# Gate and up with stationary weights in an expert layer: no transposes of the product, down right behind its own up

## The chip, the cores and the metric

One core of a Trainium2 chip runs the whole program. The metric is the device time of one launch in microseconds. TensorE is PE here (PEld are its weight loads), VectorE DVE, ScalarE ACT, GpSimd POOL, and SyncE SP, which only issues transfers.

## What is computed

```python
x = x + _L0_ffn_ref(_L0_cond_ref(x, itok_B_1_198, L0_cond_weights), gate_w, wg, wu, wd)
x = x + _L1_ffn_ref(_L1_cond_ref(x, W, A, Bm, scalings, itok_B_0_6), base_w, base_b, router_w, router_b, lora_A, lora_B)

# _L0_ffn_ref: E = 64 experts, K = 8 of them per token, H = 1024, I = 384, CAP = 256 slots per expert
probs = softmax(x @ gate_w.T);  w, sel = top_k(probs, K);  w = w / sum(w)
inp = the first CAP tokens of each expert                      # (64, 256, 1024)
h = silu(einsum('ech,ehi->eci', inp, wg)) * einsum('ech,ehi->eci', inp, wu)
out = einsum('eci,eih->ech', h, wd)
y[token] += w * out
```

x is (32, 128, 1024) in fp32: 4096 tokens. The change touches the middle part, the 64 experts; the second layer (a product W x base_w, adapters and LoRA) is only touched where it begins.

## The kernel before

Every large product is made of three: each fp32 operand is split into a high half (a copy to float32r, made by ACT) and a low half (the rest, by a subtraction on DVE), and high x high, high x low and low x high are summed in PSUM. PSUM has 8 banks of 512 fp32 columns per partition (`bank(b, a, z)`).

**Order of the program.** Routing and conditioning of 32 token tiles come first (to about 198 us into the span), then the 64 experts (to about 1886 us), then the products for the second layer and its 32 tiles. Nothing reorders at run time: each engine runs its own list in the order written, and semaphores (`wait_ge`, `then_inc`) tie the lists together. So the loops in the five blocks (`block.sync`, `gpsimd`, `tensor`, `scalar`, `vector`) are the schedule.

**Weights of an expert** come in six units of 768 KB: gA, uA, gB, uB (halves of gate and up) and dA, dB (halves of down). `stream` and `units` set their order, down's one expert behind gate and up. SP loads them into four raw buffers (`load_unit`, L305; load n waits until the low half of unit n - 4 is done). ACT's `split` (L876) copies a unit to HR (eight slots; it waits by `wait_retired`, L272, until the matmuls have used the slot's last unit), and DVE's `split` (L1176) writes the rest to LR, 1536 columns each.

**Tokens of an expert.** POOL fetches, by indirect transfers, the expert's table rows (`gather_tab`, L472, 2 transfers), its tokens (`gather_x`, L485, 8 transfers: c = 0, 1 is the half of 128 tokens, q a quarter of the columns), its routing weights (`gather_w`, 2), and adds results to the output (`scatter`, L512, 2). DVE makes token numbers (`token`, L1219) and, with a small PE matmul (`repeat`, L635), row numbers (`index`, L1195). DVE turns the gathered blocks (`turn_x`, L1182), ACT makes their high half (`high_x`, L883), DVE the low half (`low_x`, L1189). `column` (L1235) copies the routing weight out of what was gathered.

**Gate and up** (`up`, L654): for each k of 8 and each half c, six matmuls of 384 columns: the tokens (XH, XL) are stationary, the weights (HR, LR) move. The result has tokens on the partitions. ACT takes `silu` (L893), DVE multiplies (`product`, L1210). **Turning the product** (`turn_h`, L646): six PE transposes of 128 x 128 into PSUM; ACT reads the high half (`high_h`, L888), DVE the low half (`low_h`, L1203). **Down** (`down`, L681): 4 results of 9 matmuls of 512 columns, banks 4 and 5 in turn; ACT scales each into `ot` (`result`, L899). PE's order is up(e), down(e - 1), turn_h(e).

**After the experts** PE turns base_w (`turn_b`, L698, 17 steps, ACT's `high_b` and DVE's subtraction after each, L1286 to L1296), nine steps before the last down and eight behind it, and then multiplies (L751).

Of the kernel before, what the change touches and what calls it, by code (L numbers as in the profile page):

```python
# [5 lines left out]
F32 = mybir.dt.float32  # L6
# [27 lines left out]
NB0 = 9  # L34
# [18 lines left out]
def adaln_ffn_kernel(nc, x, cond, adap, w0, gate_w, wg, wu, wd, W, A, Bm, scal,  # L53
# [14 lines left out]
    with ExitStack() as ctx:  # L68
# [38 lines left out]
        hH = sb("hH", [P, 2, 3, P], F32R, moe)  # L107
        hL = sb("hL", [P, 2, 3, P], F32R, moe)
# [5 lines left out]
        sil = sb("sil", [P, 2, I], F32, moe)  # L114
        prod = sb("prod", [P, 2, 3, P], F32, moe)
# [38 lines left out]
        XH = sb("XH", [P, 2, 2, 8, P], F32R, moe)  # L154
        XL = sb("XL", [P, 2, 2, 8, P], F32R, moe)
# [66 lines left out]
        s_H, s_L, s_k, s_dn = sem("s_H"), sem("s_L"), sem("s_k"), sem("s_dn")  # L222
        s_f, s_fh, s_fl = sem("s_f"), sem("s_fh"), sem("s_fl")
# [33 lines left out]
        stream(["gA", "uA", "gB", "uB"], 0)  # L257
        for e in range(1, E):
            stream(["gA", "uA", "gB", "uB"], e)
            stream(["dA", "dB"], e - 1)  # L260
        stream(["dA", "dB"], E - 1)

        def unit_src(n):
            k, e = units[n]
            h = 0 if k[1] == "A" else UN
            if k[0] == "d":
                v = wd[e].rearrange("(p j) h -> p (j h)", j=3)
            else:
                v = (wg if k[0] == "g" else wu)[e].rearrange("(p k) i -> p (k i)", k=8)
            return v[:, h:h + UN]  # L270
# [10 lines left out]

        fq = {}
        for e in range(2):
            fq[("i", e)] = len(fq)
        for e in range(E):
            if e + 2 < E:
                fq[("i", e + 2)] = len(fq)
            for c in range(2):
                fq[("h", e, c)] = len(fq)
# [7 lines left out]
        def _(eng):  # L297
# [7 lines left out]
            def load_unit(n):  # L305
                if n >= NRAW:
                    eng.wait_ge(s_L, n - NRAW + 1)
                eng.dma_start(raw[:, n % NRAW, :], unit_src(n)).then_inc(d_raw[n % NRAW], 16)
# [136 lines left out]
        def _(eng):  # L445
# [79 lines left out]
            gather_x(0)  # L525
            gather_x(1)
            gather_tab(2)
            gather_w(0)
            gather_w(1)
            for e in range(E + 1):  # L530
                if e + 3 < E:
                    gather_tab(e + 3)
                if e + 2 < E:
                    gather_x(e + 2)
                    gather_w(e + 2)
                if e >= 1:
                    scatter(e - 1)
# [35 lines left out]
        def _(eng):  # L573
# [61 lines left out]
            def repeat(e):  # L635

                q = fq[("i", e)]
                if q >= 2:
                    eng.wait_ge(s_fl, q - 1)
# [829 lines left out]
```

## Time and profile before

| | us |
|---|---|
| median of 3 runs | 2518.43 (2515.33 to 2520.38) |
| the profiled execution's own time | 2506.1 |
| span of its trace | 2504.4 |

| engine | busy us | share of the span | instructions |
|---|---|---|---|
| PE | 2427.9 | 97% | 13439 |
| PEld | 2283.1 | 91% | 13439 |
| DVE | 1620.9 | 65% | 2673 |
| ACT | 1123.1 | 45% | 1459 |
| POOL | 1535.2 | 61% | 1044 |

Busy time is a union: two overlapping instructions of one engine count once. The mean duration of a matmul is longer than the distance to the next one's start, since they overlap; PE's pace is read from starts. "Idle before" is the time in which an engine waited, and the arrow names what ended the wait.

### The profile page before, as it was taken

To read this page: it belongs to the slowest core of one execution; us is meant where nothing else is said; L and a number is where in the kernel's file an instruction comes from. 1 tells how busy PE (TensorE), PEld (TensorE's weight loads), DVE (VectorE), ACT (ScalarE), POOL (GpSimd) and SP (SyncE) were. 2 spreads that over 40 slices of the span, in tenths; PEclk is the share of its full clock that TensorE was granted. 3 is DMA by queue.
4 is the path that set the end of the run, shared out by engine and by line. 5 is a ranking of instruction groups with operands and counts; after the bars stand their busy time and mean duration, and the time that the engine had idled before them with its cause. 6 is when DMAs were issued, how large, how long until landed. Compare 5 with 4: busy or idle time off the path is not lost.

```text
span 2504.4 us, 35281 instructions
## 1 busy us (share of the span) xinstructions
PE 2427.9 (97%) x13439; PEld 2283.1 (91%) x13439; DVE 1620.9 (65%) x2673; ACT 1123.1 (45%) x1459; POOL 1535.2 (61%) x1044
## 2 busy tenths in 40 slices
PE   8966999999999999999999999999989999999998
PEld 6756999999999999999999999999979999999998
DVE  4665777777767777776777777677732155555554
ACT  4544555555555555555555555555532121111110
POOL 4017888888888888888888888888710032223221
PEclk9987999999999999999999999999999999999999
DMA  9976999999999999899998989899964244444441
GB/s 327 355 254 241 296 273 277 263 285 263 278 289 272 278 262 284 263 280 272 269 281 263 284 262 281 271 270 280 273 154 110 68 128 132 136 129 128 126 116 52
DMA packets 216026, 583.67 MB, mean 233 GB/s; under 512 B 82793, under 2 KB 105322, under 8 KB 215730
## 3 DMA queue, kind: packets, MB, share of 16 engines
q1 hardware_dynamic: 148658, 402.26, 48.6%
q0 software_dynamic: 55808, 160.28, 26.5%
q10 hardware_dynamic: 11392, 18.88, 2.0%
q8 instruction: 107, 1.75, 0.3%
q14 instruction: 61, 0.50, 0.1%
HBM read 460.97 MB, written 124.53 MB: 234 GB/s over the span
## 4 chain that ended last, share of the span: by engine, by line
PE 88%; DMA 2%; POOL 1%; DVE 1%; SPq 1%; issue 1%; ACT 0%; DVEq 0%; POOLq 0%; ACTq 0%
PE ps L674 41%; PE ps L694 20%; PE ps L800 16%; PE ps L751 5%; PE ps L784 2%; PE ps L651 2%; POOL Xg L498 1%; PE ps L765 1%; SPq L361 1%; DMA x<-in_L_ffn_base_w 0%; DMA Xg<-yd,idx 0%; PE ps L643 0%; DMA Wg<-wdr,toki 0%; DMA G<-tabd,rowi 0%; POOL Wg L508 0%
## 5 line engine op out<-in xcount | busy, mean ns | idle before, releaser
L498 POOL DMA_INDIRECT Xg<-yd,idx x512 | 862.4, 1684 | 166.9 <-issue 138.1
L1179 DVE TENSOR_TENSOR LR<-raw,HR 128x1536 fp32r<-128x1536 f32 x384 | 666.2, 1749 | 75.1 <-ACT HR L881 74.9
L881 ACT ACTIVATE HR<-raw 128x1536 fp32r<-128x1536 f32 x384 | 563.1, 1484 | 5.9 <-PE ps L674 2.3
L674 PE MATMUL ps<-HR,XH 128*128 128x384 f32 x2048 | 531.9, 340 | 11.3 <-DVE XL L1191 11.3
L674 PE MATMUL ps<-LR,XH 128*128 128x384 f32 x2048 | 521.5, 335 | 0.0
L674 PE MATMUL ps<-HR,XL 128*128 128x384 f32 x2048 | 521.1, 335 | 0.0
L674 PEld LDWEIGHTS ps<-HR,XH 128*128 128x128 f32 x2048 | 363.7, 189 | 11.4 <-issue 11.4
L674 PEld LDWEIGHTS ps<-LR,XH 128*128 128x128 f32 x2048 | 371.0, 188 | 0.0
L674 PEld LDWEIGHTS ps<-HR,XL 128*128 128x128 f32 x2048 | 371.0, 188 | 0.0
L694 PE MATMUL ps<-HR,hL 128*128 128x512 f32 x768 | 302.5, 394 | 0.0
L694 PE MATMUL ps<-HR,hH 128*128 128x512 f32 x768 | 301.2, 392 | 0.3 <-ACT ot L904 0.3
L694 PE MATMUL ps<-LR,hH 128*128 128x512 f32 x768 | 298.3, 388 | 0.0
L520 POOL DMA_INDIRECT accd<-ot,toki x128 | 203.9, 1593 | 94.7 <-ACT ot L904 57.5
L904 ACT ACTIVATE ot<-ps,wcol 128x512 f32<-128x512 f32 x256 | 176.4, 690 | 176.7 <-PE ps L694 176.0
L885 ACT ACTIVATE XH<-XR 128x1024 fp32r<-128x1024 f32 x128 | 135.0, 1055 | 259.7 <-DVE XR L1186 259.7
L481 POOL DMA_INDIRECT G<-tabd,rowi x128 | 168.6, 1318 | 129.1 <-DMA tabd<-ct 90.4
L551 POOL DMA_INDIRECT m8a<-m8d,midx x32 | 27.6, 864 | 323.0 <-PE ps L765 322.5
L897 ACT ACTIVATE sil<-ps 128x384 f32<-128x384 f32 x128 | 55.9, 489 | 310.8 <-PE ps L674 310.8
L800 PE MATMUL ps<-MH,xTH 128*128 128x392 f32 x768 | 185.1, 349 | 3.9 <-DVE xTL L1363 3.9
L800 PE MATMUL ps<-MH,xTL 128*128 128x392 f32 x768 | 180.0, 343 | 0.0
L800 PE MATMUL ps<-ML,xTH 128*128 128x392 f32 x768 | 179.7, 342 | 0.0
L694 PEld LDWEIGHTS ps<-LR,hH 128*128 128x128 f32 x768 | 144.2, 188 | 32.2
(169 smaller groups left out, 3212.9 us busy)
## 6 DMA issues: line engine op xcount, KB each, us to landing
raw<-in_L_ffn_wg SPq DMA_DIRECT2D x128, 768.0 KB, 6.1
raw<-in_L_ffn_wu SPq DMA_DIRECT2D x128, 768.0 KB, 6.8
raw<-in_L_ffn_wd SPq DMA_DIRECT2D x128, 768.0 KB, 6.5
xt<-in_x SPq DMA_DIRECT2D x32, 512.0 KB, 7.0
yd<-yrow ACTq DMA_DIRECT2D x32, 512.0 KB, 6.6
x<-accd SPq DMA_DIRECT2D x32, 512.0 KB, 4.9
out<-osb SPq DMA_DIRECT2D x32, 512.0 KB, 3.0
accd<-xt SPq DMA_DIRECT2D x24, 512.0 KB, 6.6
```

What stands on the lines that cost most here:

```text
L481: eng.indirect_dma_start(G[:, e % 2, c, :], None, tab, bass.IndirectOffsetOnAxis(ap=rowi[:, c * E + e:c * E + e + 1], axis=0))\
L498: eng.indirect_dma_start(Xg[:, c, q, :], None, yd4, bass.IndirectOffsetOnAxis(ap=idx4[:, e % 4, i:i + 1], axis=0))\
L520: eng.indirect_dma_start(acc, bass.IndirectOffsetOnAxis(ap=toki[:, c * E + e:c * E + e + 1], axis=0), ot[:, c, :], None, compute_op=ALU.ad ...
L674: mm = eng.matmul(bank(2 * c + g, 0, I), X[:, e % 2, c, k, :], Wt[:, s, o:o + I], start=(k == 0 and m < 2), stop=(k == 7 and m >= 4))
L694: mm = eng.matmul(bank(4 + h), X[:, c, j, :], Wt[:, s, f:f + 512], start=(j == 0 and m == 0), stop=(j == 2 and m == 2))
L751: mm = eng.matmul(bank(b0 + g, 0, z - a), X[:, j % 2, q, :], Y[:, q, a:z], start=(q == 0 and m == 0), stop=(q == 7 and m == 2))
L800: mm = eng.matmul(bank(b0 + n, 0, 392), X, Y[:, k, a:a + 392], start=(k == 0 and m == 0), stop=(k == 7 and m == 2))
L881: eng.activation(HR[:, (n + 2) % NHL, :], raw[:, n % NRAW, :], ACT.Copy).then_inc(s_H, 1)
L885: eng.activation(XH[:, e % 2, c, :, :].rearrange("p j (q t) -> p q j t", q=4), XR[:, c, :, :, :], ACT.Copy).then_inc(s_vh, 1)
L897: eng.activation(sil[:, c, :], bank(2 * c, 0, I), ACT.Silu).then_inc(s_sl, 1)
L904: eng.activation(ot[:, c, h * 512:(h + 1) * 512], bank(4 + h), ACT.Copy, scale=wcol[:, c * E + e:c * E + e + 1]).then_inc(s_out, 1)
L1179: eng.tensor_tensor(LR[:, (n + 2) % NHL, :], raw[:, n % NRAW, :], HR[:, (n + 2) % NHL, :].bitcast(F32), ALU.subtract).then_inc(s_L, 1)
```

## The change

- **Gate and up.** The weights are stationary, 128 of an expert's 384 columns at a time (block b of 3), and the tokens move: XX holds, for each k, the high half of all 256 tokens beside their low half. `wh` moves all 512 columns, `wl` the 256 of the high half. Per block 2 x 8 x 2 = 32 matmuls. Gate and up use banks 0, 1 or 2, 3 in turn. The result has the inner dimension on the partitions, so `turn_h` and its six transposes are gone.
- **After a block**, n = 3e + b: ACT copies the right half of both banks (`copy_2`), DVE adds the left half (`join`), ACT takes silu, DVE multiplies (`product`), ACT makes the high half (`high_h`), DVE the low half (`low_h`), all on 128 x 256 but the first two (128 x 2 x 256).
- **Down** runs right behind its own up, its units come with it. The loop over the 3 blocks is outermost, with four banks (4 to 7) open, so that block j is wanted only at step j. down's weights are read in the order (j p) h, in runs of 512 numbers.
- **Orders.** ACT, DVE and POOL loops are rewritten; POOL's scatter(e - 1) goes ahead of gather_x(e + 2), and gather_tab(2) ahead of gather_x(1). `repeat` uses banks 4 and 5 and waits for two results of expert e - 3. The base turns of the last expert stand inside its down.

```diff
+        for e in range(E):
+            stream(["gA", "uA", "gB", "uB", "dA", "dB"], e)
...
             if k[0] == "d":
                 eng.wait_ge(s_dn, 4 * (e + 1))
             else:
-                eng.wait_ge(s_k, 2 * e + (1 if k[1] == "A" else 2))
+                eng.wait_ge(s_up, 3 * (e + 1))
...
+            gather_tab(2)
             gather_x(1)
-            gather_tab(2)
...
                 if e + 3 < E:
                     gather_tab(e + 3)
+                if e >= 1:
+                    scatter(e - 1)
                 if e + 2 < E:
                     gather_x(e + 2)
                     gather_w(e + 2)
-                if e >= 1:
-                    scatter(e - 1)
...
+            def up(e):
+                eng.wait_ge(s_vl, 2 * e + 2)
+                for b in range(3):
+                    n = 3 * e + b
+                    if n >= 2:
+                        eng.wait_ge(s_gs, n - 1)
+                    for g, kind in enumerate("gu"):
+                        out = 2 * (n % 2) + g
+                        for k in range(8):
+                            u = pos[(kind + ("A" if k < 4 else "B"), e)]
+                            if b == 0 and k % 4 == 0:
+                                eng.wait_ge(s_L, u + 1)
+                            s, o = (u + 2) % NHL, (k % 4) * I + b * P
+                            wh, wl, xx = HR[:, s, o:o + P], LR[:, s, o:o + P], XX[:, e % 2, k, :]
+                            if k == 0:
+                                eng.matmul(bank(out), wh, xx, start=True, stop=False)
+                                eng.matmul(bank(out, 0, CAP), wl, xx[:, 0:CAP], start=False, stop=False)
+                            else:
+                                eng.matmul(bank(out, 0, CAP), wl, xx[:, 0:CAP], start=False, stop=False)
+                                mm = eng.matmul(bank(out), wh, xx, start=False, stop=(k == 7))
+                        if g == 0 and b == 0 and 0 < e < E - 2:
+                            repeat(e + 2)
+                    mm.then_inc(s_up, 1)
...
+            def down(e):
+                eng.wait_ge(s_fl, min(e + 3, E))
+                eng.wait_ge(s_L, pos[("dB", e)] + 1)
                 for j in range(3):
+                    eng.wait_ge(s_hl, 3 * e + j + 1)
+                    for o in range(4):
+                        c, h = divmod(o, 2)
+                        if j == 0 and e:
+                            eng.wait_ge(s_out, 4 * (e - 1) + o + 1)
+                        s = (pos[("dA" if h == 0 else "dB", e)] + 2) % NHL
+                        for m, (X, Wt) in enumerate([(hH, HR), (hL, HR), (hH, LR)]):
+                            mm = eng.matmul(bank(4 + o), X[:, j, c * P:(c + 1) * P], Wt[:, s, j * 512:(j + 1) * 512],
+                                            start=(j == 0 and m == 0), stop=(j == 2 and m == 2))
+                        if j == 2:
+                            mm.then_inc(s_dn, 1)
+                        if e == E - 1 and j >= 1:
+                            turn_b(8 * (j - 1) + 2 * o)
+                            turn_b(8 * (j - 1) + 2 * o + 1)
...
             for e in range(E):
                 up(e)
-                if e >= 1:
-                    down(e - 1)
-                for c in range(2):
-                    turn_h(e, c)
...
+            def copy_2(n):
+                eng.wait_ge(s_up, n + 1)
+                if n:
+                    eng.wait_ge(s_hp, n)
+                b0 = 2 * (n % 2)
+                eng.activation(gu[:, :, :], ps[:, b0:b0 + 2, CAP:2 * CAP], ACT.Copy).then_inc(s_c2, 1)
+
+            def silu(n):
+                eng.wait_ge(s_gs, n + 1)
+                eng.activation(sil[:, :], gu[:, 0, :], ACT.Silu).then_inc(s_sl, 1)
+
+            def high_h(n):
+                e, b = divmod(n, 3)
+                eng.wait_ge(s_hp, n + 1)
                 if e:
+                    eng.wait_ge(s_dn, 4 * e)
+                eng.activation(hH[:, b, :], prod[:, :], ACT.Copy).then_inc(s_hh, 1)
...
+            split("dA", 0)
+            for e in range(E):
+                split("dB", e)
+                if e + 1 < E:
+                    high_x(e + 1, 0)
+                    high_x(e + 1, 1)
+                copy_2(3 * e)
+                silu(3 * e)
+                high_h(3 * e)
                 if e + 1 < E:
                     split("gA", e + 1)
                     split("uA", e + 1)
+                for b in (1, 2):
+                    copy_2(3 * e + b)
+                    silu(3 * e + b)
+                    high_h(3 * e + b)
+                if e + 1 < E:
                     split("gB", e + 1)
                     split("uB", e + 1)
+                    split("dA", e + 1)
+                    for o in range(4):
+                        result(e, o // 2, o % 2)
...
+            def join(n):
+                b0 = 2 * (n % 2)
+                eng.wait_ge(s_c2, n + 1)
+                eng.tensor_tensor(gu[:, :, :], ps[:, b0:b0 + 2, 0:CAP], gu[:, :, :], ALU.add).then_inc(s_gs, 1)
+
+            def product(n):
+                eng.wait_ge(s_sl, n + 1)
+                if n:
+                    eng.wait_ge(s_hh, n)
+                eng.tensor_tensor(prod[:, :], sil[:, :], gu[:, 1, :], ALU.mult).then_inc(s_hp, 1)
+
+            def low_h(n):
+                eng.wait_ge(s_hh, n + 1)
+                eng.tensor_tensor(hL[:, n % 3, :], prod[:, :], hH[:, n % 3, :].bitcast(F32), ALU.subtract)\
+                   .then_inc(s_hl, 1)
...
+            split("dA", 0)
+            for e in range(E):
+                split("dB", e)
                 if e + 1 < E:
                     turn_x(e + 1, 0)
                     turn_x(e + 1, 1)
+                if 0 < e < E - 2:
+                    index(e + 2)
+                join(3 * e)
+                product(3 * e)
+                low_h(3 * e)
+                if e == 0:
+                    column(0)
+                if e + 1 < E:
+                    column(e + 1)
+                    low_x(e + 1, 0)
+                    low_x(e + 1, 1)
                     split("gA", e + 1)
...
+                join(3 * e + 1)
+                product(3 * e + 1)
+                low_h(3 * e + 1)
...
+                if e + 1 < E:
                     split("uA", e + 1)
+                if e + 3 < E:
+                    token(e + 3)
+                join(3 * e + 2)
+                product(3 * e + 2)
+                low_h(3 * e + 2)
+                if e + 1 < E:
                     split("gB", e + 1)
                     split("uB", e + 1)
+                    split("dA", e + 1)
```

## Rows read from the trace of the kernel before

**Rows 1.** The page, part 1: busy us, share of the span, instructions.
```profile
PE 2427.9 (97%) x13439; PEld 2283.1 (91%) x13439; DVE 1620.9 (65%) x2673; ACT 1123.1 (45%) x1459; POOL 1535.2 (61%) x1044
```

**Rows 2.** Stretches: length, busy us of PE, PEld, DVE, ACT, POOL, clock, DMA, GB/s.
```profile
700.00:1100.00 400.00, 400.00 (x2176) 376.66 (x2175) 296.40 (x371) 226.47 (x248) 333.85 (x218) 1.00 0.91 274
...
1858.00:1863.00 5.00, 3.83 (x21) 3.56 (x20) 3.35 (x7) 2.52 (x5) 0.00 (x0) 0.66 1.01 232
```

**Rows 3.** Waits, 700 to 1500 us: total us, times, longest.
```profile
DVE idx L1198 <- PE ps L643: 85.0, 31, 2.7
...
DVE prod L1214 <- ACT sil L897: 43.5, 31, 1.4
```

**Rows 4.** Timeline of PE: start us, us, line, operation, shape, count.
```profile
1205.13 0.39 PE L694 MATMUL ps<-HR,hH 128*128 128x512 f32 x1
...
1209.26 0.82 PE L651 MATMUL ps<-ident,prod 128*128 128x128 f32 x6
...
1210.26 0.51 PE L674 MATMUL ps<-LR,XH 128*128 128x384 f32 x2
...
1211.65 0.51 PE L674 MATMUL ps<-HR,XL 128*128 128x384 f32 x2
...
1235.05 0.82 PE L651 MATMUL ps<-ident,prod 128*128 128x128 f32 x6
```

**Rows 5.** Timeline of PE in the second layer, LoRA's three groups of three matmuls.
```profile
2123.28 0.63 PE L784 MATMUL ps<-lbH,mgH 128*128 128x392 f32 x3
...
2124.69 0.69 PE L800 MATMUL ps<-MH,xTH 128*128 128x392 f32 x3
```

**Rows 6.** Groups by form outside the experts: count, busy us, mean ns, idle before.
```profile
L1294 DVE TENSOR_TENSOR BL<-ps,BH 128x512 fp32r<-128x512 f32 x16 | 10.4, 688 | 16.6 <-ACT BH L918 16.6
...
L918 ACT ACTIVATE BH<-ps 128x512 fp32r<-128x512 f32 x16 | 9.0, 602 | 10.3 <-PE ps L713 10.3
...
L1403 DVE TENSOR_TENSOR mg<-ps,gate 128x128 f32<-128x128 f32 x32 | 9.3, 291 | 1.1
```

**Rows 7.** Groups by form, 700 to 1500 us.
```profile
L498 POOL DMA_INDIRECT Xg<-yd,idx x248 | 427.0, 1722 | 75.6 <-issue 66.4 <-ACT ot L904 9.1
...
L904 ACT ACTIVATE ot<-ps,wcol 128x512 f32<-128x512 f32 x124 | 85.6, 690 | 85.1 <-PE ps L694 84.8 <-issue 0.3
...
L885 ACT ACTIVATE XH<-XR 128x1024 fp32r<-128x1024 f32 x63 | 66.5, 1055 | 117.2 <-DVE XR L1186 117.2
```

**Rows 8.** Timelines of ACT (first row) and DVE: start us, us, count, idle before.
```profile
170.37 5.60 ACT L881 ACTIVATE HR<-raw 128x1536 fp32r<-128x1536 f32 x4 [1.46 <-issue]
...
1214.74 2.37 DVE L1186 STREAM_TRANSPOSE XR<-Xg 128x1024 f32<-128x1024 f32 x2
...
1222.61 3.42 DVE L1179 TENSOR_TENSOR LR<-raw,HR 128x1536 fp32r<-128x1536 f32 x2
...
1230.96 0.34 DVE L1222 TENSOR_SCALAR_CACHE_REDUCE Gj<-G,slot 128x128 f32<-128x128 f32 x1
...
1232.18 0.19 DVE L1231 TENSOR_TENSOR tokq<-qm,tokf 128x8 f32<-128x8 f32 x1
```

**Rows 9.** Timeline of POOL.
```profile
1222.68 2.50 POOL L498 DMA_INDIRECT Xg<-yd,idx  x1 [0.30 <-issue]
...
1228.41 0.94 POOL L498 DMA_INDIRECT Xg<-yd,idx  x1 [0.30 <-issue]
```

**Rows 10.** Transfers by line: count, KB each, median us from issue to landing.
```profile
raw<-in_L_ffn_wd SPq DMA_DIRECT2D x128, 768.0 KB, 6.5
...
x<-in_L_ffn_base_w SPq DMA_DIRECT2D x8, 512.0 KB, 6.9
x<-in_L_cond_W SPq DMA_DIRECT2D x32, 128.0 KB, 3.9
```

**Rows 11.** Timeline of PE: up of the last expert, and the W product.
```profile
1828.36 0.60 PE L674 MATMUL ps<-HR,XH 128*128 128x384 f32 x2
...
1886.08 1.31 PE L751 MATMUL ps<-BH,WH 128*128 128x392 f32 x3 [3.05 <-DVE WL L1302]
```

More of the change, by code:

```diff
@@ L106, in adaln_ffn_kernel @@
         rt0.close()
[L107 to L108 removed]
+        hH = sb("hH", [P, 3, CAP], F32R, moe)
+        hL = sb("hL", [P, 3, CAP], F32R, moe)
         ot = sb("ot", [P, 2, D], F32, moe)
@@ L720, in _ @@
                 up(e)
-                if e >= 1:
-                    down(e - 1)
-                for c in range(2):
-                    turn_h(e, c)
-            for n in range(NB0):
-                turn_b(n)
-            down(E - 1)
-            for n in range(NB0, 17):
-                turn_b(n)
+                down(e)
+            turn_b(16)
             eng.wait_ge(s_bl, 18)
@@ L903, in result @@
                 eng.wait_ge(s_dn, 4 * e + 2 * c + h + 1)
-                eng.activation(ot[:, c, h * 512:(h + 1) * 512], bank(4 + h), ACT.Copy,
+                eng.activation(ot[:, c, h * 512:(h + 1) * 512], bank(4 + 2 * c + h), ACT.Copy,
                                scale=wcol[:, c * E + e:c * E + e + 1]).then_inc(s_out, 1)
-            for k in ("gA", "uA", "gB", "uB"):
-                split(k, 0)
-            for c in range(2):
-                high_x(0, c)
             def high_b(n):
@@ L919, in high_b @@
                                    bank(n % 4).rearrange("p (q n) -> p q n", q=4), ACT.Copy).then_inc(s_bh, 1)
-            for e in range(E + 1):
-                if e >= 1:
-                    high_h(e - 1, 0)
-                    high_h(e - 1, 1)
-                if e == E:
-                    eng.wait_ge(s_k, 2 * E)
-                    eng.wait_ge(d_la, 16 * 16)
-                    eng.activation(BH[:, :, D + NA:NX], laR[:, :, :, :].rearrange("p q a r -> p q (a r)"), ACT.Copy)\
-                       .then_inc(s_bh, 1)
-                    for n in range(NB0):
-                        high_b(n)
+            for k in ("gA", "uA", "gB", "uB"):
+                split(k, 0)
@@ L937, in _ @@
                     split("gB", e + 1)
                     split("uB", e + 1)
-                if e < E:
-                    silu(e, 0)
-                    silu(e, 1)
-                    split("dA", e)
-                if e >= 1:
-                    result(e - 1, 0, 0)
-                    result(e - 1, 0, 1)
-                if e < E:
-                    split("dB", e)
-                if e >= 1:
-                    result(e - 1, 1, 0)
-                    result(e - 1, 1, 1)
-            for n in range(NB0, 17):
-                high_b(n)
+                    split("dA", e + 1)
@@ new lines, in _ @@
+                    for o in range(4):
+                        result(e, o // 2, o % 2)
+            eng.wait_ge(d_la, 16 * 16)
+            eng.activation(BH[:, :, D + NA:NX], laR[:, :, :, :].rearrange("p q a r -> p q (a r)"), ACT.Copy)\
+               .then_inc(s_bh, 1)
+            for n in range(8):
+                high_b(n)
+            for o in range(4):
+                result(E - 1, o // 2, o % 2)
+                high_b(8 + 2 * o)
+                high_b(9 + 2 * o)
+            high_b(16)
@@ L1250, in _ @@
                 low_x(0, c)
-            for e in range(E + 1):
-                if e >= 1:
-                    low_h(e - 1, 0)
-                    low_h(e - 1, 1)
-                if e >= 1 and e + 2 < E:
-                    index(e + 2)
+            split("dA", 0)
+            for e in range(E):
+                split("dB", e)
                 if e + 1 < E:
```

165 lines of the change are left out of this document (39 added, 126 removed).

## The prediction

> **What bounds the kernel now.** The page comes first: TensorE is busy for 97% of the span [rows 1]. That alone doesn't say that it is full, since matmuls overlap, so I read the stretches: in 400 us of the experts' stage PE is busy for all 400 at full clock, DVE for 74%, ACT for 57%, POOL for 83% [rows 2]. Then the waits: over 31 experts no wait of PE is listed at all, while DVE waits 85 us for PE [rows 3]. PE's timeline gives the beat: from one group of transposes to the next 25.79 us [rows 4], the same for nearly all 64. Starts are 0.229 us apart at 512 columns (18 steps from 1205.13 to 1209.26), 0.174 at 384 (8 from 1210.26 to 1211.65), about 0.109 at 128 (six in the 0.65 below). An expert is 96 x 0.174 + 36 x 0.229 = 24.94, the transposes 0.65 (they and two matmuls of 0.174 fill the 1.00 from 1209.26 to 1210.26), the token matmul the rest, 0.2: 25.8. PE bounds, with ACT and DVE in its shadow.
>
> **What PE's own work becomes.** Columns stay the same: 48 matmuls of 512 and 48 of 256 in place of 96 of 384. 256 columns don't occur before. Nearest is LoRA's group of three, 392 + 392 + 240 columns in 0.47 us (2123.28 to 2124.69 is three of them) [rows 5]; with 0.179 for 392 that leaves 0.112 for 240. The line through 384 and 512 gives 0.119. I take 0.116; the far bound is 0.188, a whole weight load with nothing over it (rival 2). Gate and up: 48 x (0.229 + 0.116) = 16.56, 0.14 less. The six transposes go, 0.65 less. PE alone: **25.0 us** per expert, 0.75 less than now. That's the whole gain on offer; a perfect cover gives 64 x 0.75 = 48 us.
>
> **What is put on ACT and DVE.** Per expert the change removes two silus and two high parts of 384, two products and two low parts of 384. It adds, for each of three blocks, a chain that changes engine at every step: copy (ACT, 512 from PSUM, 0.60), join (DVE, 512 with PSUM, 0.69) [rows 6], silu, product, high, low on 256. ACT at 256: from 1.055 at 1024 [rows 7] and 1.48 at 1536, 0.84 ns a column, so 0.41. DVE at 256: between 0.291 at 128 and 0.688 at 512 [rows 6], 0.42. A hand-over costs 0.04, as where a split waits for ACT and starts at once. An instruction that waits for nothing starts before its forerunner's end: four ACT splits take 5.60, so 1.37 apart; two DVE splits 3.42, so 1.67 apart; two turns of x 2.37 [rows 8]. I take 0.11 off for ACT and 0.08 for DVE.
>
> Each block's chain is therefore 0.73 + 0.45 + 0.46 + 0.45 = 2.09 from join to the end of the high part, with DVE idle for 0.9 of it, since silu and high run on the other engine and the queues are in order. What matters is what stands **between** the chains. Following the two queues round once, each released by the one before:
> - ACT, after block 2's high part: splits gB, uB, dA of the next expert, 3 x 1.37 = 4.12. They can't be earlier: their slots retire with the last up matmul, and they are queued behind this chain.
> - ACT: four results, 4 x 0.58 = 2.32 (0.69 less overlap [rows 7]). Down ends just before, so they go in a row instead of in PE's shadow.
> - ACT split dB 1.52; DVE split dB 1.67 and two turns 2.41: 5.60.
> - ACT: second high part of x 0.94 and copy 0.64: 1.58.
> - Block 0: 2.09, its low part 0.34: 2.43.
> - DVE: column 0.09, two low parts of x 2.27 (1024 columns, 1.22 by the slope above), split gA 1.67: 4.03.
> - Block 1: 2.43.
> - DVE: split uA 1.67, token 1.33 (1230.96 to 1232.37 [rows 8]): 3.00.
> - Block 2 to its high part: 1.94.
>
> Sum 27.45 us. **The ring of ACT and DVE is 2.4 longer than PE's 25.0 and 1.67 longer than the present beat.** PE waits in down, at j = 2 before the first matmul, for block 2's low part; behind it stand the rest of down and the next expert's up. Before, down ran an expert late, so this chain had up's 16.7 us of cover; now only two thirds of down, 5.5 us, are between up's end and the need, and block 2's join stands in DVE behind block 1, uA and token.
>
> **Other moved steps.** Times here count from up's start; the ring puts its first result at 0.6. SP's loads still wait for the low split four units back. With the ring above, the tightest is dB: issued when uA's low part ends (20.7 after up's start), needed at 30.3; at 6.5 to landing [rows 10] 3 us are left. Down's weights now come in runs of 2 KB, 384 per unit against 128. A quarter of W's slice, 1024 runs of 128 bytes, lands in 3.9 [rows 10], so 256 more runs cost at most 1 us: nothing, by that cover; without it 1 us per expert. The indirect scatter is moved ahead of the next gathers in POOL's queue; results come 1 to 3 us into up and the two scatters end near 8, where the gathers wait anyway for the turns and the index (8.6). Gathers then land some 8 us before their turn. The token matmul's new wait for two results ends a microsecond before its place. PSUM join and copy run on different banks than PE's next block, whose wait for join(n-2) is just met (10.8 against 11.3).
>
> **Ends.** Start: the first up needs both halves of x, four gathers more at 1.25 each [rows 9], less what overlapped: +4; the first column copies now stand ahead of the low parts of x and wait for POOL's late weights: +5. So +9 (4 to 14). Tail: up 63 starts at 1828.4 and the W product at 1886.1 [rows 11], 57.7 us with down 62 and stalled base turns between. After, down 62 is done, up and two thirds of down take 20 to 22, and 17 turns spread into down go at DVE's 0.60 and wait for the last loads (6.9 to landing); I get 38: -20. The last two experts have no next x: -2.6.
>
> **Sum.** 61 beats x 1.67 = +102, +9, -20, -2.6: **+88 us**. The profiled execution took 2506.1 (span 2504.4), which becomes 2594; the median shown, 2518.4, is 12.3 above it, so 2606. Terms: the ring is 26.7 if join and the 256-wide forms are 0.07 to 0.09 cheaper, and 28.5 if handovers cost 0.08 and results and splits don't overlap. So 2561 to 2671.
>
> **Rivals.** (1) **Faster: PE stays the bound at 25.0.** For it: DVE's own work is only about 21 us and ACT's 19, so both fit; if a few links (results, dB, the turns) don't wait as I have them, the ring opens. Against: the queues are written in that order, and today DVE visibly waits 1.4 us per expert for silu alone [rows 3]. Since start and tail give 14 back, it is faster as soon as the beat is under 26.0, 1.45 less than my sum. At 25.0: 2518 + 61 x (-0.75) - 14 = 2459. Half way, near 2500.
> (2) **Weight loads show behind 256 columns.** 48 x (0.229 + 0.188) + 8.45 = 28.5 per expert, PE then bound again: 2670. Against: 128 columns run 0.109 apart, each with its own load [rows 4].
> (3) **POOL bounds.** Its 14 indirect transfers fill the beat now, gaps of 0.30 being all its idle time. They take 0.94 alone, but 2.50 when they start under DVE's split, ending 0.82 after the split does [rows 8, 9]. Products and low parts now read SBUF twice like the split: six more of 0.42, at most 2.5 us more per expert: 28.3, or about 2658. The Trainium skill (GPSIMD Engine Reference, Specifications) says that GpSimd shares its SBUF interfaces with VectorE and contends with DVE instructions that have two SBUF inputs; the trace agrees for the split, and by this rule the added ones speak against the change. Against: today's gathers stretch by what they happen to meet, 1.72 on the mean [rows 7] of 0.94 to 2.50, and six short ones seldom meet.
> (4) **PE's clock falls** during the new wait. It stood at 0.66 on the mean, so part of the time at 1.2 GHz, in 5 us of base turns with PE idle for 1.2 of them [rows 2]. If down's last third, 2.75 us, then takes twice that, +2.75 per expert: about 2770.
>
> **Chances.** Ring 0.62; PE bound or nearly (1) 0.22; (2) 0.04; (3) 0.06; (4) 0.06. Below 2490 I leave 0.12, above 2670 some 0.08, so the range is 2490 to 2670. A measurement here can tell 0.2% (5 us) from no change. Faster 0.22, same 0.03, slower 0.75.
>
> **What would show it.** Beat 27.4 from up to up; PE idle 2.4 us per expert, all in down, released by the low part hL on DVE; PE's share falls to about 91%; silu on ACT waits for the join three times; the four results run in a row about 0.5 us into the next up; POOL has idle time again. Starts of 256 columns 0.11 to 0.12 apart. It is wrong if PE lists no wait for hL, if its wait sits at up for the join or for a split (then the order of links is another), or if POOL's gathers release the turns.

## The result, and the profile after

The changed kernel takes **2613.04 us** (median of 4 runs, 2612.15 to 2618.15), the kernel before 2518.4 us beside it on the same chip (4 runs). The ratio is **1.0381** (95% interval 1.0363 to 1.0399): slower, by 94.6 us. Forecast were 2606, a ratio of 1.0348. The profiled execution took 2612.15, its span is 2610.4.

The page of the changed kernel, part 1, answers [rows 1].

```profile
PE 2437.0 (93%) x13055; PEld 2126.5 (81%) x13055; DVE 1732.6 (66%) x2993; ACT 1258.5 (48%) x1779; POOL 1470.4 (56%) x1044
```

The stretches of the experts' stage answer [rows 2]: length, busy us of PE, PEld, DVE, ACT, POOL, then clock, DMA share, GB/s.

```profile
700.00:1100.00 400.00, 374.62 (x1962) 315.91 (x1961) 301.78 (x427) 241.30 (x305) 297.04 (x206) 1.00 0.87 260
1100.00:1500.00 400.00, 379.16 (x1958) 318.78 (x1957) 300.56 (x418) 244.81 (x307) 299.37 (x203) 0.98 0.83 256
```

PE was busy for all 400 us and now is for 375. No other engine has taken its place: DVE stands at 75% where it had 74%, ACT at 60%, and POOL fell from 83% to 74%. When every engine has room and the beat is longer, the bound is a chain that passes between engines. The waits from 700 to 1500 us answer [rows 3] (total us, times, longest).

```profile
ACT sil L875 <- DVE gu L1190: 131.8, 61, 3.6
ACT XX L863 <- DVE XR L1170: 89.4, 30, 3.0
POOL accd L511 <- ACT ot L889: 60.9, 29, 3.1
PEld ps L674 <- DVE hL L1200: 55.7, 27, 2.4
PE ps L674 <- DVE hL L1200: 44.0, 27, 1.9
DVE LR L1163 <- ACT HR L857: 39.7, 30, 1.3
DVE prod L1196 <- ACT sil L875: 39.2, 81, 0.5
POOL Xg L489 <- DVE idx L1182: 36.4, 30, 1.2
```

TensorE, which had no wait here at all, now waits in every expert at line 674 (down): 27 times in these 800 us for the low part of h, 1.6 us on the mean and at most 1.9, and twice more with no releaser named. The timeline of ACT over one beat (start us, us, idle before) shows the order in which its queue goes round.

```profile
1102.07 4.22 ACT L857 ACTIVATE HR<-raw 128x1536 fp32r<-128x1536 f32 x3
1106.19 2.40 ACT L889 ACTIVATE ot<-ps,wcol 128x512 f32<-128x512 f32 x4
1108.47 1.49 ACT L857 ACTIVATE HR<-raw 128x1536 fp32r<-128x1536 f32 x1
1112.95 2.19 ACT L863 ACTIVATE XX<-XR 128x1024 fp32r<-128x1024 f32 x2 [2.98 <-DVE XR L1170]
1115.04 0.58 ACT L871 ACTIVATE gu<-ps 128x512 f32<-128x512 f32 x1
...
1129.20 0.42 ACT L882 ACTIVATE hH<-prod 128x256 fp32r<-128x256 f32 x1 [0.49 <-DVE prod L1196]
1129.53 1.47 ACT L857 ACTIVATE HR<-raw 128x1536 fp32r<-128x1536 f32 x1
```

DVE's timeline over the same beat:

```profile
1110.00 1.76 DVE L1163 TENSOR_TENSOR LR<-raw,HR 128x1536 fp32r<-128x1536 f32 x1 [1.34 <-ACT HR L857]
1111.67 2.36 DVE L1170 STREAM_TRANSPOSE XR<-Xg 128x1024 f32<-128x1024 f32 x2
...
1115.65 0.69 DVE L1190 TENSOR_TENSOR gu<-ps,gu 128x512 f32<-128x512 f32 x1 [1.50 <-ACT gu L871]
1116.83 0.42 DVE L1196 TENSOR_TENSOR prod<-sil,gu 128x256 f32<-128x256 f32 x1 [0.49 <-ACT sil L875]
1117.73 0.42 DVE L1200 TENSOR_TENSOR hL<-prod,hH 128x256 fp32r<-128x256 f32 x1 [0.48 <-ACT hH L882]
1118.08 0.16 DVE L1221 COPY wcol<-Wg 128x2 f32<-128x2 f32 x1
1118.15 2.35 DVE L1176 TENSOR_TENSOR XX<-XR,XX 128x1024 fp32r<-128x1024 f32 x2
1120.42 1.75 DVE L1163 TENSOR_TENSOR LR<-raw,HR 128x1536 fp32r<-128x1536 f32 x1
1122.09 0.68 DVE L1190 TENSOR_TENSOR gu<-ps,gu 128x512 f32<-128x512 f32 x1
...
1124.58 1.76 DVE L1163 TENSOR_TENSOR LR<-raw,HR 128x1536 fp32r<-128x1536 f32 x1
...
1127.58 0.68 DVE L1190 TENSOR_TENSOR gu<-ps,gu 128x512 f32<-128x512 f32 x1
```

Read from start to start, each link released by the one before, this is the forecast's ring, the chain that goes once round the queues of ACT and DVE in each expert: three splits on ACT 4.12; four results 2.28; split dB on ACT 1.53 to DVE's start, on DVE 1.67, and the two turns up to ACT's second high part 2.40, together 5.60; high part and copy to the join 1.58; block 0 2.43; column, two low parts, split gA 4.01; block 1 2.49; split uA and the token 3.00; block 2 to the end of its high part 1.95. **Sum 27.46 us**, from ACT's split at 1102.07 to its next at 1129.53. The beat from up to up is 27.42 on the mean of the 61 from expert 2 to expert 63.

PE's timeline (answers [rows 4]) shows its own pace, and its wait:

```profile
1105.53 0.40 PE L652 MATMUL ps<-XX,HR 128*128 128x512 f32 x1
1105.76 0.28 PE L653 MATMUL ps<-XX,LR 128*128 128x256 f32 x1
1105.88 0.27 PE L655 MATMUL ps<-XX,LR 128*128 128x256 f32 x1
1105.99 0.40 PE L656 MATMUL ps<-XX,HR 128*128 128x512 f32 x1
...
1130.13 0.50 PE L674 MATMUL ps<-HR,hH 128*128 128x512 f32 x1 [1.94 <-DVE hL L1200]
```

512 columns are followed after 0.23 us, 256 after 0.11 to 0.12. From 700 to 1500 us, at full clock, the means in up are 0.234 and 0.116.

Where the time went, span against span (2610.4 - 2504.4 = +106.0): the routing phase of that one execution +13.2 (first token matmul at 199.96 against 186.8, in code that the change leaves alone); the first up, counted from there, +3.6; expert 0 to expert 2, 66.8 against 57.9, +8.9; 61 beats, 1672.6 against 1572.5, +100.1; from the last up to the W product 37.7 against 57.7, -20.0; the rest +0.2.

### The profile page after: what moved, and what is told of

Its sections match the earlier page's. It is cut to its first block, busy times and chain, and to the rows that moved or that the text cites. A ratio compares the mean times of both kernels' runs of the same rounds, so it can differ in the third digit from the quotient of the medians.

```text
span 2610.4 us, 35529 instructions
## 1 busy us (share of the span) xinstructions
PE 2437.0 (93%) x13055; PEld 2126.5 (81%) x13055; DVE 1732.6 (66%) x2993; ACT 1258.5 (48%) x1779; POOL 1470.4 (56%) x1044
## 4 chain that ended last, share of the span: by engine, by line
PE 33%; ACT 22%; DVE 21%; issue 15%; DMA 1%; POOL 1%; ACTq 0%; DVEq 0%; POOLq 0%
PE ps L776 16%; ACT HR L857 10%; PE ps L674 8%; DVE XR L1170 5%; ACT ot L889 5%; PE ps L727 4%; DVE LR L1163 4%; DVE prod L1196 3%; DVE gu L1190 3%; ACT sil L875 3%; ACT gu L871 2%; DVE hL L1200 2%; ACT hH L882 2%; PE ps L760 2%; PE ps L656 2%
## 5 line engine op out<-in xcount | busy, mean ns | idle before, releaser
L656 PE MATMUL ps<-XX,HR 128*128 128x512 f32 x2688 | 961.2, 397 | 0.0
L489 POOL DMA_INDIRECT Xg<-yd,idx x512 | 677.3, 1323 | 227.0 <-issue 137.2
L655 PE MATMUL ps<-XX,LR 128*128 128x256 f32 x2688 | 751.5, 280 | 0.0
L656 PEld LDWEIGHTS ps<-XX,HR 128*128 128x128 f32 x2688 | 506.5, 188 | 104.5
L655 PEld LDWEIGHTS ps<-XX,LR 128*128 128x128 f32 x2688 | 508.7, 189 | 17.5
L511 POOL DMA_INDIRECT accd<-ot,toki x128 | 287.5, 2246 | 201.1 <-ACT ot L889 181.6
L674 PEld LDWEIGHTS ps<-HR,hH 128*128 128x128 f32 x768 | 148.7, 194 | 146.7 <-DVE hL L1200 115.0
L863 ACT ACTIVATE XX<-XR 128x1024 fp32r<-128x1024 f32 x128 | 136.0, 1063 | 224.2 <-DVE XR L1170 213.6
L1190 DVE TENSOR_TENSOR gu<-ps,gu 128x512 f32<-128x512 f32 x192 | 131.3, 684 | 104.3 <-ACT gu L871 102.8
L674 PEld LDWEIGHTS ps<-HR,hL 128*128 128x128 f32 x768 | 149.6, 195 | 32.3
```

Source lines behind the costliest of these rows:

```text
L489: eng.indirect_dma_start(Xg[:, c, q, :], None, yd4, bass.IndirectOffsetOnAxis(ap=idx4[:, e % 4, i:i + 1], axis=0))\
L511: eng.indirect_dma_start(acc, bass.IndirectOffsetOnAxis(ap=toki[:, c * E + e:c * E + e + 1], axis=0), ot[:, c, :], None, compute_op=ALU.ad ...
L655: eng.matmul(bank(out, 0, CAP), wl, xx[:, 0:CAP], start=False, stop=False)
L656: mm = eng.matmul(bank(out), wh, xx, start=False, stop=(k == 7))
L674: mm = eng.matmul(bank(4 + o), X[:, j, c * P:(c + 1) * P], Wt[:, s, j * 512:(j + 1) * 512], start=(j == 0 and m == 0), stop=(j == 2 and m ...
L863: eng.activation(XX[:, e % 2, :, c * P:(c + 1) * P].rearrange("p j (q t) -> p q j t", q=4), XR[:, c, :, :, :], ACT.Copy).then_inc(s_vh, 1)
```

## The experiments

Times are compared by the ratio to the kernel before on the same chip, since that kernel took 2503, 2505, 2516 and 2519 us beside the four sets. The difference lies ahead of the experts: beside 2503 and 2505 the first up starts at 200 to 204 us, beside 2516 and 2519 at 213 to 214. "Beat" is the mean distance from up to up over experts 2 to 63; "the first two" is the stretch from the up of expert 0 to that of expert 2. The theory is the forecast's ring; the main rival was that PE, the weight loads or POOL set the beat.

### The changed kernel again (c0_after)

> The changed kernel once more, with no edit, so that the others of this call have it beside them on the same chip. Ratio to the kernel before 1.038, a beat of 27.4 us from up to up in the experts, and the same rows as in the first trace.

Measured: ratio 1.0372 (1.0352 to 1.0392), 2599.18 us; beat 27.41, first two 66.9. The size holds on a second chip.

### More work for TensorE (e1_more_pe)

```diff
                             if k == 0:
+                                if g == 0:
+                                    for _ in range(2):
+                                        eng.matmul(bank(out), wh, xx, start=True, stop=True)
                                 eng.matmul(bank(out), wh, xx, start=True, stop=False)
```

The two extra products are overwritten by the next matmul.

> Adds to each block of up two matmuls of 512 columns that the next start=True overwrites: 6 x 0.233 = 1.4 us more PE work per expert. Ring of ACT and DVE sets the beat: beat stays 27.47, PE's wait for hL shrinks from 2.4 to about 1.0 us, time 2613 +0 to +10 us. PE (or its weight loads) sets the beat: +1.4 x 64 = +90, 2703 us. Clock theory (PE loses time because its clock falls in the wait): shorter waits, no falls, so a few us less than 2613.

Measured: ratio 1.0394 (1.0376 to 1.0411), beat 27.41. The stretch of 400 us and the wait of PE in it:

```profile
700.00:1100.00 400.00, 391.70 (x2036) 329.59 (x2035) 301.97 (x424) 242.62 (x305) 296.53 (x204) 1.00 0.85 258
```
```profile
PE ps L677 <- DVE hL L1203: 8.3, 15, 0.6
```

PE is busy for 17 of the 400 us more than in the first trace, the wait for hL shrinks from at most 1.9 to at most 0.6, and the beat doesn't move. PE isn't the bound, and neither are its weight loads, of which it had six more per expert. Nor is the clock the cause: in this trace it stays at full speed from expert 1 to the last, with the beat unchanged.

### A longer link (e2_silu_twice)

```diff
+                eng.activation(sil2[:, :], gu[:, 0, :], ACT.Silu)
                 eng.activation(sil[:, :], gu[:, 0, :], ACT.Silu).then_inc(s_sl, 1)
```

> ACT takes each silu twice (the first into a spare tile): 3 x 0.31 = 0.93 us more ACT work per expert, inside the chains. Ring: every link adds, beat 28.4, 64 x 0.93 = +59, 2672 us. If ACT's spare time (it is busy for 60% of the stage) covered it, or PE set the beat: 2613 +-5. POOL sets the beat: 2613 +-5.

Measured: ratio 1.0605 (1.0587 to 1.0623), beat 28.30, that is +0.88 for 3 x 0.31 = 0.93 us put in. ACT was at 60% and had room for the work many times over; what counts is that it stands in the ring. In 400 us POOL's busy time fell from 297 to 258 us while the kernel got slower, which it could not if it were what the others wait for.

### A shorter one on DVE (e3_token_later)

```diff
-                if e + 3 < E:
-                    token(e + 3)
                 join(3 * e + 2)
                 product(3 * e + 2)
                 low_h(3 * e + 2)
+                if e + 3 < E:
+                    token(e + 3)
```

> token(e + 3) on DVE goes from ahead of block 2's chain to behind it, where DVE waits 0.95 us for ACT's split anyway. Ring: up to 1.33 us less per expert; the same recurrence over the queues gives a beat of 26.4, so 61 x 1.05 = -64, about 2550 us, and PE waits 1.35 for hL. DVE's sum of work sets the beat: no change, 2613, since the work only moves. POOL: no change or slower, since token numbers come later.

Measured: ratio 1.008 (1.0063 to 1.0096), beat 26.18, where the recurrence gave 26.4. The beat falls by 1.23, nearly the whole 1.32 us that the token takes in the timeline: behind block 2 it lies in the time in which DVE waits for ACT's splits.

### A shorter one at the turns (e4_turns_first, e10_one_turn)

e4 moves both turns of the next tokens ahead of DVE's split dB, e10 only the first:

```diff
             for e in range(E):
-                split("dB", e)
                 if e + 1 < E:
                     turn_x(e + 1, 0)
                     turn_x(e + 1, 1)
+                split("dB", e)
```

> DVE turns the next expert's x before it splits dB instead of after. Then the turns don't stand behind four results and ACT's split of dB. Ring: that link (results 2.3, split dB 1.5) leaves the ring, which falls below PE's work: beat 25.1 (PE's own), PE waits for nothing, 61 x 2.4 = -146, about 2467 us, faster than the kernel before (2518). If turning early makes DVE wait for POOL's gathers instead: DVE waits on Xg, beat 26 to 27.5, 2520 to 2613 us. If gates other than the ring hold the beat: 2613.

> The changed kernel with only the first of the two turns of x ahead of VectorE's split dB (e4 moved both, and TensorE became the bound before the whole gain could be seen). Theory (both turns are links of the ring, 1.16 us each): one leaves it, and neither TensorE nor another chain takes over yet: a beat of 27.41 - 1.16 = 26.25 us, 63 x 1.16 = 73 us below the control's, a ratio of 1.008. Rival (the link that counted was the second turn with the high part behind it, which stays where it is): 1.037 as the control.

Measured: e4 0.9844 (0.9827 to 0.986), beat 25.24, **faster than the kernel before**; e10 1.0089 (1.007 to 1.0108), beat 26.28. One turn is a link of 1.13 us. The stretches of e4 and of e10:

```profile
700.00:1100.00 400.00, 400.00 (x2122) 342.24 (x2121) 326.22 (x462) 266.49 (x333) 296.03 (x222) 1.00 0.90 281
```
```profile
700.00:1100.00 400.00, 388.06 (x2041) 327.35 (x2040) 315.66 (x440) 252.05 (x320) 305.76 (x212) 1.00 0.89 269
```

In e4 PE is busy throughout again and no wait of PE is listed from 700 to 1100 us; POOL is at 74% as in the changed kernel, though the beat is 2.2 us shorter.

### Is TensorE the bound in e4? (e5_turns_first_more_pe)

The edits of e4 and e1 together.

> e4 (the two turns of the next expert's x ahead of VectorE's split dB) with e1's two extra matmuls of 512 columns in each up block: 6 x 0.233 = 1.4 us of TensorE work per expert. In e1 these cost nothing, because TensorE waited 1.9 us in each expert. Theory (with the turns first TensorE is the bound, its beat of 25.24 us in e4 being its own work): the beat becomes 25.24 + 1.4 = 26.6 us and the time 63 x 1.4 = 88 us over e4's, a ratio of about 1.02 to the kernel before. Rival (a ring of VectorE and ScalarE of about 25.2 us still sets e4's beat, and TensorE is only near it): less than half of it shows, under 44 us, a ratio below 1.002. What is measured is set beside e4's ratio of 0.984 from the call before.

Measured: ratio 1.0177 (1.0157 to 1.0198), beat 26.61 against 25.24: +1.37 for six matmuls, 0.228 each, all of it shown. The same six that cost nothing in e1 cost their full price here. So 25.24 is PE's own work per expert.

### A shorter one on ACT (e7_results_after_dB)

```diff
             for e in range(E):
-                split("dB", e)
+                if e == 0:
+                    split("dB", 0)
...
                     split("dA", e + 1)
+                    split("dB", e + 1)
                     for o in range(4):
                         result(e, o // 2, o % 2)
```

The recurrence that the expectation names starts each queued instruction at the end of its forerunner or of its releaser, whichever is later, with the durations of the trace.

> Only ScalarE's order is changed: its half of split dB of the next expert is issued ahead of the four copies of results instead of behind them. Theory (the ring runs through the four results of 2.32 us, because split dB stands behind them on ScalarE and holds VectorE's two turns): the results leave the ring, which falls from 27.4 to some 26 us, less than the 2.32 us because another chain comes next: the recurrence over the queues gives a beat of 25.9 us with TensorE waiting about 0.9 us for a result buffer ahead of down's first matmuls. Time 63 x 1.5 = 95 us below the changed kernel's, a ratio of about 1.00. Rival (the ring runs through VectorE alone, its own 20 us of work and POOL's copies between): no change, 1.038. Second rival (TensorE's wait for a free result bank becomes longer than the one removed): above 1.038.

Measured: ratio 1.0045 (1.0029 to 1.0062), beat 26.06, 1.35 of the 2.3 us. PE's waits from 700 to 1100 us:

```profile
PE ps L634 <- issue: 6.6, 12, 2.1
```

The wait for hL is gone from PE's own list. PE now stands at `repeat` (line 634), which the change makes wait for two results of the expert before. The expectation had the new wait, but ahead of down's first matmuls. "issue" is the profile's word where it finds no releaser; that it is this wait, and that it is what keeps the other 0.9 us, is inferred from the code and was not tested.

### POOL's order (e6_scatter_last, e11_scatter_between)

e6 puts the scatter behind the gathers again, where the kernel before has it; e11 puts it between gather_x and gather_w.

```diff
-                if e >= 1:
-                    scatter(e - 1)
                 if e + 2 < E:
                     gather_x(e + 2)
                     gather_w(e + 2)
+                if e >= 1:
+                    scatter(e - 1)
```

> The changed kernel with POOL's old order: scatter(e-1) behind gather_x(e+2) and gather_w(e+2) instead of ahead of them. Theory (the ring of ScalarE and VectorE sets the beat and POOL has slack: it stood idle ahead of the scatter and of the gathers in each expert): the beat stays 27.4 us, since the gathers start no earlier than their index, and the scatter ends well before the next results need its buffer: ratio 1.037 as the control's (1.035 to 1.040). Rival (POOL's order mattered, the scatter ahead of the gathers delays the next tokens, part of the loss): the beat falls by up to the scatter's 2 x 1.3 us. Other rival (the scatter last holds up the results, which are in the ring): the beat rises, by up to as much.

Measured: ratio **1.2874** (1.2847 to 1.2901), 3239.12 us, beat 37.66. Theory and first rival are wrong; the last rival has the sign, with 10.2 us per expert where it gave at most 2.6. The timelines of e6, POOL and then ACT, DVE and PE:

```profile
1107.26 1.62 POOL L511 DMA_INDIRECT accd<-ot,toki  x1 [0.30 <-issue]
1109.18 2.36 POOL L511 DMA_INDIRECT accd<-ot,toki  x1 [0.31 <-issue]
...
1129.48 0.94 POOL L489 DMA_INDIRECT Xg<-yd,idx  x1 [13.88 <-DVE idx L1182]
...
1146.94 2.36 POOL L511 DMA_INDIRECT accd<-ot,toki  x1 [0.31 <-issue]
```
```profile
1121.24 2.42 ACT L889 ACTIVATE ot<-ps,wcol 128x512 f32<-128x512 f32 x4 [10.19 <-DMA accd<-ot,toki]
```
```profile
1125.07 1.76 DVE L1163 TENSOR_TENSOR LR<-raw,HR 128x1536 fp32r<-128x1536 f32 x1 [11.64 <-ACT HR L857]
...
1129.03 0.18 DVE L1182 TENSOR_SCALAR idx<-ps,f 128x8 int32<-128x8 f32 x1
```
```profile
1122.61 0.56 PE L634 MATMUL ps<-tokq,rep 128*128 128x8 f32 x2 [9.33 <-issue]
```

There is a second ring, through POOL. The results of expert e may be written only when the scatter of e - 1 has landed (`ot` is one buffer). ACT's split dB stands behind the results, DVE's split dB and the turns behind that, and the index of a later token list behind the turns. With the scatter behind gather_x, each scatter also waits for that index. `repeat` waits for two results too, and PE stands 9.3 us before it, up to 1122.61, but the ring doesn't pass through it: the index comes only at 1129.03, right behind the turns. Its length from these rows: gathers, Wg and scatter from 1129.48 to the end of the next pair of scatters at 1149.30, 19.8; landing 9.7 (1111.54 to 1121.24); results and split dB 3.8; DVE's split, turns and index up to POOL's start 4.4: 37.7.

Read off the code, and not tested: in the kernel before, the same steps (results, ACT's split dB, DVE's, index, gathers, scatter) lead from one scatter to the next but one, so they had two beats of time.

> e6 with the scatter one step forward: behind gather_x(e+2), but ahead of gather_w(e+2). In e6 the beat rose to 37.66 us. Theory (a second ring closed there, through POOL: index on VectorE, eight gathers of x 13.0 us, two of Wg 2.5, the scatter with 10.7 to its landing, results on ScalarE, split dB, turns, index again, and each step stands in the time of the one before): without the two Wg transfers, 0.95 + 0.30 us each, in the ring the beat is 37.66 - 2.5 = 35.2 us. Rival (it is not this ring, but for instance slower transfers with the scatter's traffic beside the loads): the beat stays 37.7 or falls back to 27.4.

Measured, one run: 2823.09 us, beat 30.90, 6.8 us less than in e6 where 2.5 were expected. The same steps in e11, POOL and then ACT:

```profile
1117.37 1.62 POOL L511 DMA_INDIRECT accd<-ot,toki  x1 [0.31 <-issue]
1119.29 1.57 POOL L511 DMA_INDIRECT accd<-ot,toki  x1 [0.30 <-issue]
...
1134.57 0.94 POOL L489 DMA_INDIRECT Xg<-yd,idx  x1 [6.47 <-DVE idx L1183]
```
```profile
1126.32 2.42 ACT L890 ACTIVATE ot<-ps,wcol 128x512 f32<-128x512 f32 x4 [2.66 <-DMA accd<-ot,toki]
```

The landing took 5.5 us (1120.86 to 1126.32) in place of 9.7, and the second scatter 1.57 in place of 2.36. With 2.5 for Wg, 0.8 and 4.2 make 7.5; this stretch of e11 has a beat of 30.25, 7.4 below e6. Over 700 to 1500 us the landing takes 9.5 us on the mean in e6 (8.1 to 10.0 in 21 experts) and 6.1 in e11 (5.3 to 8.4 in 26): 3.4, 0.8 and 2.5 make 6.7 of the 6.8. SP's queue tells why it may be so: in e6 three weight loads of 768 KB are issued at 1110.12, 1111.79 and 1113.45, from 1.4 us before the end of the scatter to 1.9 after it; in e11 they come at 1122.72, 1124.39 and 1126.06, 1.9 to 5.2 us after it. So loads run beside the landing in both, but start later in e11. That they are what delays it is not shown: it rests on this comparison.

### The first expert (e8_early_token2, e9_first_expert)

In the changed kernel PE stood 11.3 us inside the first expert, in `repeat(2)`, for DVE's token list. e8 is e4 with that list made before the loop:

```diff
             split("dA", 0)
+            token(2)
             for e in range(E):
...
-                if 0 < e < E - 2:
+                if e < E - 2:
                     index(e + 2)
...
-                if e == 0:
-                    token(2)
...
-                if e == 0:
-                    index(2)
```

> e4, with the token list of expert 2 turned and split ahead of expert 0's work on VectorE instead of behind its first product, and index(2) with the others. Theory (in the changed kernel TensorE stood 11.3 us in the first expert, in the repeat of expert 2's token list, for VectorE's token list): that wait goes, and little is late in its place: the stretch from expert 0 to expert 2 falls from e4's 65.0 us to about 55, and the whole from a ratio of 0.984 to about 0.980. Rival (what stands behind it, the first high and low parts of h, is then late by as much, since VectorE has the same work before it): 0.984 as e4, the stretch still near 65 us.

e9 adds, for expert 0, block 0's chain ahead of the turns on DVE (and ahead of the high parts of x on ACT), and takes the repeat into block 0:

```diff
+                if e == 0:
+                    join(0)
+                    product(0)
+                    low_h(0)
                 if e + 1 < E:
                     turn_x(e + 1, 0)
                     turn_x(e + 1, 1)
...
-                        if g == 0 and b == 0 and 0 < e < E - 2:
+                        if g == 0 and b == 0 and e < E - 2:
                             repeat(e + 2)
```

> e8, with expert 0 put in order too: VectorE's join, product and low part of block 0 ahead of the turns of expert 1's x, whose gathers land late there (VectorE stood 4.0 us for them in e8 with the join behind), ScalarE's copy, silu and high part likewise, and the repeat of expert 2's token list inside block 0 as for every other expert (in e8 VectorE stood 2.4 us for it). Theory (the 7.6 us that the stretch from expert 0 to expert 2 still has over two beats are those stops): about 5 of them go, the stretch is 52 to 54 us, the rest as e8, a ratio of about 0.980. Rival (the tokens of expert 1 are the cause and come no earlier): 58 us and 0.982 as e8.

Measured: e8 0.9817 (0.98 to 0.9834), first two 58.1 against e4's 65.0; e9 0.9815 (0.9801 to 0.9829), first two 56.4. e8's gain of 6.9 in the trace, of the 10 expected, is there, though the intervals of e4 and e8 overlap; e9's 1.7 is too small for a ratio to show, and a third of what was expected. What is left over two beats of 25.24 in e9 is partly clock. Its first stretch in up(0), behind a wait of 14.3 us for the tokens, the next, and a later one behind short waits:

```profile
213.70:218.00 4.30, 4.30 (x15) 3.73 (x16) 3.01 (x9) 1.43 (x2) 3.38 (x4) 0.56 0.51 136
218.00:222.00 4.00, 4.00 (x25) 3.54 (x24) 0.00 (x0) 0.45 (x1) 3.09 (x4) 1.00 0.95 370
...
231.20:234.50 3.30, 2.94 (x9) 2.22 (x9) 2.82 (x3) 0.78 (x2) 2.83 (x2) 0.50 0.96 363
```

15 matmuls in 4.3 us, then 25 in 4.0: the granted clock stood at 0.56, most of it at 1.2 GHz, and about 2 of the 5.9 us are that. The third stretch, at 1.2 GHz throughout, costs up to 1.5 more (an estimate: half of the 2.9 us in which PE was busy there). The rest stays open.

## Why the prediction was right

**The ring, the main term.** Forecast 27.45 us, measured 27.46 in the trace and 27.42 as the mean beat. Link by link the largest error is 0.06 (block 1, 2.49 against 2.43); the group of split dB and turns came out at 5.60 as worked out. That it is a cause and not a coincidence of sums is shown by changing links one at a time: +0.93 put into silu gave +0.88, a turn taken out gave -1.13, the token moved gave -1.23, and 1.4 us of work on PE, outside the ring, gave 0. The results gave -1.35 of 2.28, as another wait took over.

**TensorE's own work.** Forecast 25.0, measured 25.24 in e4, where e5 shows it to be PE's. 256 columns take the 0.116 of the forecast; up's 512 take 0.234 in place of 0.229, so the 48 pairs are 16.8 for 16.56, and this is the miss of 0.24 (down's 36 x 0.229 and the token matmul's 0.2 make up the rest). The gain on offer was 0.54 us a beat, not 0.75. The wait of PE was forecast as 2.4 and is listed as up to 1.9; 27.42 - 25.24 gives 2.2, the list counting from the modelled end of the last matmul. It sat where it was put: in down, at the block that needs hL. PE's busy share of a stretch fell to 94% (375 of 400 us), not to the 91% named as a sign.

**The last experts and the tail.** 61 beats with the shorter last ones +100.1, forecast 102 - 2.6 = 99.4. Tail -20.0, forecast -20 (37.7 us, forecast 38).

**The start was mis-sized.** Forecast +9, measured 3.6 + 8.9 = 12.5 in the trace. The step that failed is "the first column copies now stand ahead of the low parts of x and wait for POOL's late weights: +5". Those copies wait for nothing: no idle time stands before them in DVE's timeline, the first row. What PE stood for is the token list of expert 2, in `repeat(2)`, and POOL's next gathers waited for its index, as the waits from 205 to 290 us show:

```profile
234.25 0.23 DVE L1221 COPY wcol<-Wg 128x2 f32<-128x2 f32 x2
```
```profile
POOL Xg L489 <- DVE idx L1182: 12.1, 1, 12.1
...
PE ps L634 <- DVE tokq L1215: 11.3, 1, 11.3
```

DVE makes that list behind expert 0's first chain, low parts of x and split gA, and before these it stood for the late tokens of expert 1. e8, which moves only that list, takes 6.9 us off e4. The other term, +4 for the first up, came out at 3.6.

**What was costed at nothing.** The down weights in another order, the added waits and the later loads: no wait of PE for a weight is listed from 700 to 1500 us. The scatter's move was costed at nothing too, which is what it costs. But the reasoning was only half there: it looked at what the scatter would delay, not at what the old place would have done now that the index stands behind ACT's results and split dB of the same beat. e6 shows 10 us per expert: the move isn't an option but a condition of the new order.

**The rivals.** (1) PE as the bound is false for this kernel and true for e4: it takes one swap in DVE's queue, and the point named for it (faster below a beat of 26.0) agrees with e4 at 25.24 (0.984) and with e7 and e3 at 26.06 and 26.18, just above it (1.0045 and 1.008). (2) Weight loads behind 256 columns don't show: 0.116, and 0.188 was the bound. (3) POOL: its busy share fell, and it idles ahead of the scatters (60.9 us in 800) and the gathers (36.4). Products and low parts didn't stretch it into a bound: from 700 to 1500 us the 58 gathers that start under a product take 1.00 us on the mean (0.94 to 1.20), where 30 that start under nothing take 1.02. The one at 1120.49, under a split, still takes 2.50, but in time that nobody waits for. The Trainium skill (GPSIMD Engine Reference, Specifications) says that GpSimd contends with two-input DVE instructions. The trace agrees for the split; for the product these means show nothing of it. (4) The clock did fall, in both traces of this kernel, and it cost nothing in the experts (last section).

**The total.** 2606 against 2613. The start's 3.5 and the beats' 0.7 are 4 of the 7 us; the other 3 stay open. The profiled executions differ by 106.0, the medians by 94.6, since the routing phase took 13.2 longer in one profile than in the other, as it does between the sets above. That is about the 12.3 us by which the forecast went up from the profiled execution to the median.

## What to carry to other kernels

A chain that crosses two engines several times per round is costed by following both queues round once and adding every instruction that stands between its links, its own or not; busy shares of 75% and 60% hid a ring that was 2.2 us longer than TensorE's work. Then look for what stands between links without being one, and move that first: two turns moved ahead of one subtraction turned 3.8% slower into 1.6% faster, with the same work on the same engines. And before a reordering is called harmless, ask which ring its old place would close: one swap in POOL's queue cost 24%, through a single output buffer and a transfer that must land.

## What the hardware did that was not expected

**A clock that falls at no price.** In the changed kernel the granted clock fell to half behind PE's wait of 1.9 us, in some runs of experts in every second one, in others in none. Behind the wait that ends at 1130.13 a window of the first trace reads:

```profile
1131.60:1134.00 2.40, 2.40 (x7) 1.92 (x6) 2.40 (x2) 2.40 (x3) 2.01 (x1) 0.50 0.27 55
```

That is 1.2 GHz, 7 matmuls in 2.4 us. The beats there alternate, 29.0 and 25.9, and their sum is that of two of 27.46. The second trace of the same kernel (c0) has such falls too, in other experts:

```profile
706.50:709.80 3.30, 3.30 (x9) 2.63 (x8) 3.30 (x3) 3.30 (x4) 2.20 (x1) 0.50 0.39 94
```

In e1, where PE waits at most 0.6, the clock doesn't fall there at all, and all three have the same mean beat, 27.42, 27.41 and 27.41. So the falls cost nothing here. PE had slack, so its slower matmuls came out of the next wait. Where it had none, as behind the wait at the start (e9), the half clock cost about 2 us. Rival (4) of the forecast, 2.75 us in each expert, had left that slack out.

**A scatter that lands slowly.** From the end of POOL's instruction to the release of ACT it is 9.5 us on the mean in e6, where three weight loads are issued around that end, and 6.1 in e11, where they come 1.9 us after it and later.
